# Six of seven key groups of the later pairs staged split and turned by VectorE

## What is computed

```python
qp = jnp.einsum('bsd,de->bse', q, Wq) + bq        # q = layernorm(x), (8, 64, 512)
kp = jnp.einsum('bsd,de->bse', k, Wk) + bk        # k = v = ctx_1024, (8, 1601, 512)
vp = jnp.einsum('bsd,de->bse', v, Wv) + bv
logits = jnp.einsum('bqe,bke->bqk', qp, kp) * scale
attn = jax.nn.softmax(logits, axis=-1)
return jnp.einsum('bqk,bke->bqe', attn, vp)
```

## Time and profile before

| | |
|---|---|
| median of three runs | 350.5 us |
| profiled execution | 349.09 us, span 347.4 us, mean granted clock 0.986 |
| TensorE matmul busy | 315.8 us (91%), 1940 instructions |
| VectorE busy | 161.4 us (46%), 349 instructions |
| ScalarE busy | 89.1 us (26%) |
| GpSimd busy | 77.6 us (22%) |
| moved by DMA | 74.29 MB in 61221 packets, 214 GB/s over the span |
| packets under 2 KB | 40070 |

### The profile page before, as it was taken

How to read it: one execution, slowest core, us unless ns; L and a number is a source line. 1 busy time by engine, 2 the same in 40 slices (tenths; PEclk the granted TensorE clock), 3 DMA queues, 4 the chain that set the end, 5 groups by cost and what they waited for, 6 DMA issues and landing times. The chain is left out here.

```text
span 347.4 us, 5470 instructions
## 1 busy us (share of the span) xinstructions
PE 315.8 (91%) x1940; PEld 174.8 (50%) x1940; DVE 161.4 (46%) x349; ACT 89.1 (26%) x207; POOL 77.6 (22%) x84
## 2 busy tenths in 40 slices
PE   0997988999999899999899999999999998789992
PEld 0786654743545544454554454543475577433330
DVE  3205149505463857183767437442362647034331
ACT  1233210145113463221335321152312501011010
POOL 4000012660015200221500201321325210601212
PEclk9999998899999999999999999999999999999998
DMA  7999999999999897999796999680696053730110
GB/s 252 387 351 176 184 372 359 190 190 364 298 197 300 166 158 255 298 196 354 109 169 106 352 245 234 231 358 0 235 422 252 0 184 123 222 141 31 44 41 9
DMA packets 61221, 74.29 MB, mean 214 GB/s; under 512 B 3174, under 2 KB 40070, under 8 KB 60176
## 3 DMA queue, kind: packets, MB, share of 16 engines
q1 hardware_dynamic: 59648, 69.23, 75.8%
q0 software_dynamic: 1552, 4.78, 3.9%
HBM read 70.85 MB, written 3.67 MB: 215 GB/s over the span
## 5 line engine op out<-in xcount | busy, mean ns | idle before, releaser
L1182 PE MATMUL ST<-CTX_sb,PR_sb 128*64 128x512 f32 (+1 forms) x208 | 47.7, 599 | 1.1 <-ACT PR_sb L338 1.1
L784 DVE STREAM_TRANSPOSE CT_sb<-FF_sb 128x1024 f32<-128x1024 f32 x36 | 42.4, 1220 | 11.6 <-DMA FF_sb<-ctx 10.0
L1157 PE MATMUL SC<-CT_sb,qcurP_sb 128*64 128x256 f32 x288 | 38.6, 398 | 3.3 <-DVE CT_sb L784 3.3
L1157 PEld LDWEIGHTS SC<-CT_sb,qcurP_sb 128*64 128x64 f32 x288 | 19.2, 140 | 17.9 <-issue 7.3
L1182 PEld LDWEIGHTS ST<-CTX_sb,PR_sb 128*64 128x64 f32 (+1 forms) x208 | 14.1, 136 | 24.3 <-issue 23.5
L1082 PE MATMUL A<-AW_sb,normT_sb 128*128 128x512 f32 x48 | 22.0, 600 | 0.0
L511 POOL TENSOR_TENSOR rn_sb<-ss_sb,nhalf_sb 128x16 f32<-128x16 f32 x4 | 11.6, 2905 | 35.9 <-DVE ss_sb L863 35.9
L1075 PE MATMUL TR<-ident_sb,CTX_sb 128*128 128x128 f32 (+1 forms) x128 | 15.9, 266 | 1.3 <-DVE CT_sb L331 1.1
L1125 PE MATMUL A<-AO_sb,WQK_sb 128*128 128x128 f32 (+1 forms) x64 | 16.2, 413 | 0.7 <-ACT AO_sb L611 0.7
L1075 PEld LDWEIGHTS TR<-ident_sb,CTX_sb 128*128 128x128 f32 (+1 forms) x128 | 12.9, 141 | 7.5 <-issue 5.6
L1326 PE MATMUL SC<-ident_sb 128*128 128x128 f32 x130 | 16.4, 278 | 0.0
(11 more groups left out here) (242 smaller groups left out, 489.9 us busy)
## 6 DMA issues: line engine op xcount, KB each, us to landing
CTX_sb<-ctx SPq DMA_DIRECT2D x24, 1024.0 KB, 10.4
FF_sb<-ctx SPq DMA_DIRECT2D x80, 128.0 KB, 6.9
FF_sb<-ctx SPq DMA_DIRECT2D x32, 256.0 KB, 8.0
CTX_sb<-wgu SPq DMA_DIRECT2D x4, 1024.0 KB, 9.6
CTX_sb<-wdn SPq DMA_DIRECT2D x5, 512.0 KB, 12.6
FF_sb<-wgu SPq DMA_DIRECT2D x2, 1024.0 KB, 6.2
rows<-XR_sb SPq DMA_DIRECT2D x3, 512.0 KB, 10.3
CTX_sb<-ctx SPq DMA_DIRECT2D x8, 130.0 KB
```

The source lines that it names most:

```text
L784: v.transpose(ctxT[:, pos % 2, k, :, :].rearrange("p c (b r) -> p b c r", r=Q), split[:, k, at:at + BLOCKS, :].rearrange("p b (c r) -> p b ...
L1157: last = t_.matmul(out[q, :], (qcurP if split_group else qcur)[:, c, q], ctxT[:, pos % 2, k, c, 0:n], start=(c == 0), stop=(c == DC - 1))
L1182: last = t_.matmul(ST[q, :], probs[0:w, t, q], ctxb[0:w, k, t, :], start=(t == 0), stop=(t == KT - 1))
```

## The change

The later pairs take the groups in the order 0 to 6, and group 0 is split too: only the tail is turned by TensorE. The slot of a group is its number modulo three. The first pair keeps three split and four unsplit groups, renumbered: 3, 4, 5, 6 unsplit, then 0, 1, 2 split, and its chunks 0 and 1 swap their places in the loads. Before a pair, groups 0 and 1 are loaded when all but the last split group of the pair before are turned, group 2 when that one is turned too; in `load_pair`, groups 3 and 4 are issued where 4 and 5 were, then chunk 3, then, once group 2 is turned, group 5 in a part of its own, and chunk 2 last.

```diff
-SLOT_OF = {1: 0, 2: 1, 3: 2, 4: 0, 5: 1}
-SPLIT_PARTS = ((1, 2), (3,), (4,), (5,))
+SLOT_OF = {0: 0, 1: 1, 2: 2, 3: 0, 4: 1, 5: 2}
+SPLIT_PARTS = ((0, 1), (2,), (3,), (4,), (5,))
...
-FIRST = Order((0, 4, 5, 6, 1, 2, 3), (1, 2, 3))
-NEXT = Order((1, 2, 0, 3, 4, 5, 6), (1, 2, 3, 4, 5))
+FIRST = Order((3, 4, 5, 6, 0, 1, 2), (0, 1, 2))
+NEXT = Order((0, 1, 2, 3, 4, 5, 6), (0, 1, 2, 3, 4, 5))
...
             def next_split(p):
 
-                sp.wait_ge(s["keysT_made"], split_turned(p, order_of(p).split.index(3) + 1))
+                done = len(order_of(p).split)
+                sp.wait_ge(s["keysT_made"], split_turned(p, done - 1))
+                settle(sp)
+                load_split(p + 1, 0)
+                sp.wait_ge(s["keysT_made"], split_turned(p, done))
                 settle(sp)
                 load_split(p + 1, 1)
-                sp.wait_ge(s["keysT_made"], split_turned(p, len(order_of(p).split)))
-                settle(sp)
-                load_split(p + 1, 0)
...
                 load_split(p, 2)
                 load_split(p, 3)
                 load_chunk(p, 3)
+                sp.wait_ge(s["keysT_made"], split_turned(p, 3))
+                settle(sp)
+                load_split(p, 4)
                 load_chunk(p, 2)
...
-            for c in (0, 2, 3):
+            for c in (1, 2, 3):
                 load_chunk(0, c)
...
-            load_chunk(0, 1)
+            load_chunk(0, 0)
```

## The result

The changed kernel took 357.4 us (median of 4 runs, 354.1 to 359.8) against 350.1 us for the kernel before on the same chip: ratio 1.015, 95% interval 1.009 to 1.021. The medians and ranges of this document are of all runs, while a ratio is of the runs within 1.5% of the fastest of their kernel, here without the one of 359.8 us. The changed kernel is slower; whether by as much as 2% is open. A second measurement of the same kernel gave 358.5 us and 1.020 (1.015 to 1.026). The profiled execution took 357.34 us, its span is 355.6 us, 8.2 more than before.

A forecast was written before the change was run, and what follows sets the result against it. TensorE was taken as the bound from 60 to 235 us. Terms 3.3 + 1.2 + 0.6 + 0.8 + 1.5 = +7.4 on the profiled 349.1 gave 356.5; with 1.4 for the median 357.9, forecast 358, range 352.5 to 363.

The forecast's parts named there:

- the three transfer terms: Later pairs' loads: group 3 late +1.2, gates and what follows +0.6, group 5 late +0.8 us.
- Removed transposes: TensorE, tiles 0 and 1 of three pairs: 16 transposes a pair fewer, 2.0 us a pair, 6.0 us in all.
- The chain y, turn, statistics, a2: VectorE's group 2 turn between x1 and statistics delays a2: +1.1 us a pair, +3.3 over three pairs.
- Late group 3: First later pair: VectorE waits 3.6 us for group 3, normT follows, TensorE waits for q: +1.2 us.
- the gates behind it: First later pair: group 4's turn delays q's squares, k norm and gates, then group 5 and resonance steps: about +0.6 us.
- TensorE is through the v projection at 102.1: First later pair: step by which TensorE, done with v at 102.1, waits for q until 103.3: +1.2 us.
- Late group 5: Group 5's own part behind the tail chunk lands about 224 us in the third pair, TensorE waits: +0.8 us.
- The clock, one fall: New TensorE waits, 3.2 us idle in 4.2 a pair, bring one half-clock fall: +1.5 us (none to 4.5).
- The edits costed at nothing: First pair's renumbering, chunk 2 issued some 7 us later, earlier load of next pair's first two groups: no cost.
- B: Rival: only the chain costs, transfers land early enough and the clock holds: 353.8 us, chance 0.17.
- C: Rival: clock falls in every pair, or group 3 is late in later pairs too: 361 us, chance 0.18.
- D: Rival: a2 chain has room, removed transposes count in full; a2 must be 2 us plus turn old: 344.5, chance 0.10.

The follow-up runs named there:

- experiment 8: Experiment 6's kernel with SyncE issuing chunk 2 only behind the next pair's groups 0 and 1: 347.91 us, ratio 0.989 to the kernel before.
- experiment 10: Changed kernel with only the load order new (parts ahead of chunks 0 and 1, chunk 2 behind the next pair's groups): 355.16 us, ratio 1.013.
- Experiment 2: Kernel before plus four stream transposes of 128x512 into dead buffers on VectorE, behind y in the later pairs: 357.53 us, ratio 1.018.
- experiment 1: Changed kernel with VectorE turning the group at position 2 ahead of y: 355.57 us, ratio 1.014 to the kernel before.
- experiment 3: Changed kernel without group 5's loads and the waits for them (its scores are wrong): 355.05 us, ratio 1.013 to the kernel before.
- experiment 5: Changed kernel with 4 and 6 filler matmuls in TensorE's two waits: 359.12 us, ratio 1.021; changed kernel again beside it: 358.54 us, 1.020.
- experiment 6: Experiment 1's kernel with the parts of groups 3, 4, 5 and the tail issued ahead of chunks 0 and 1: 350.41 us, ratio 0.998.
- experiment 4: Changed kernel with 10 and 14 filler matmuls of 128x128 in TensorE's two waits of each later pair: 361.70 us, ratio 1.031.
- experiment 9: Experiment 8's kernel with TensorE scoring the second half of group 2 ahead of the transpose of a2: 348.87 us, ratio 0.989.

## Why the prediction was right

Forecast 358, measured 357.4; the profiled sum was +7.4, measured +8.2. The total is nearer than its terms, and that is partly luck: the chain came out as forecast, the three transfer terms (2.6 us) cost TensorE nothing in the profiled execution, and the clock cost 4.2 us there instead of 1.5.

- **Removed transposes, 6.0 us.** Right: 48 fewer, 42 stream transposes. Experiments 8 and 10 show what they are worth once the chain is out of the way and the loads are in time.
- **The chain y, turn, statistics, a2: +3.3.** Right in mechanism and size. Forecast: waits of 1.35 and 1.85 us, a2 on TensorE 5.8 us after x1, +1.1 a pair. Measured: 1.19, 1.65 (once 1.72), 5.8 us (97.48 against 91.72), +1.04 to +1.11. Experiment 2 puts about the same work there without the change and loses 1.9 a pair; experiment 1 moves it away and turns +1.04 into −1.1 up to a2; experiments 3 and 10 keep it with less or earlier traffic, and it stays.
- **Late group 3 and the gates behind it, +1.2 and +0.6.** In the profiled execution VectorE's wait was there (2.83 us instead of 3.6, and 2.00 more for group 4), but its effect on TensorE was not: the step that failed is "TensorE is through the v projection at 102.1". At half clock it was through at 105.5. In the filled kernel's execution of experiment 5, which began early and held the clock, both waits appeared (1.01 and 1.14 us), in experiment 1 too (0.72 and 1.03 us), and in the second profile of the changed kernel, which began late, neither. So the terms belong to some executions and not to all.
- **Late group 5, +0.8.** Not in the first profile (0.56 us of waiting, 0.63 before), where SyncE issued the part in 5.08 us and I had taken 7.3: I priced its issues by half of a stretch of sixteen that stood behind two whole chunks. It was there in the second profile (1.51 us), where SyncE took 6.23 us, and at its worst in experiment 1 (2.54 us).
- **The clock, one fall, +1.5.** Mis-sized: two falls, 2.8 and 1.4 us, in the first profile; none in the pairs in the second and in experiment 3; one of 2.8 in experiment 10. The Trainium skill, TensorE: Matmul & The Clock Gate, What's actually happening, has idleness as the trigger. The traces agree that falls follow the waits; nothing in them says why the same two waits (1.19 and 1.65 us) brought one in 3 of the 12 pairs of these four profiles and not in the others. The row that the forecast took its one fall from was no surer: the same wait of 2.08 us in the first pair brought a fall in the kernel before and none in the changed one, as TensorE's timelines show, before and after. Why stays open.

```profile
53.22 2.40 PE L1157 MATMUL SC<-CT_sb,qcurP_sb 128*64 128x256 f32 x16 [2.08 <-DVE CT_sb L784]
```

```profile
53.88 1.95 PE L1161 MATMUL SC<-CT_sb,qcurP_sb 128*64 128x256 f32 x16 [2.08 <-DVE CT_sb L788]
```

- **The edits costed at nothing.** The first pair's renumbering and chunk 2's later issue left no wait in the profiles of the changed kernel; the 0.6 us ahead of the first start are within what that start varies by, so whether the renumbering has a part in them is not shown.
- **Rivals.** B (only the chain, 353.8) describes the pairs of experiment 3, whose median is 3.7 us above its kernel before, and of experiment 10 but for the clock. C (the clock in every pair) happened in no profiled execution. D (faster) fell at the point named for it: a2 was not 2 us old. Yet its amount was partly to be had, once the turn was moved and the loads put in another order: the removed work was real, and the place of what replaced it ate it.

In the median, the loss is 5 to 7 us (by the ratio 1.015 and by the medians); 3.1 of it are the chain; the other 2 to 4 are what is left, and by the profiles they are clock falls and late transfers. How these two divide could not be settled, since the slow clock hides the late transfer: TensorE at half clock came to q only when normT was there.

## What to carry to other kernels

When work is moved from the bound engine to one with time to spare, look not at its busy share but at the instruction behind which it will stand and at the chain that it delays; 2.36 us in the one place between x1 and the statistics cost more than the 2.0 us of TensorE that it saved, in each of three pairs. If the order is at fault, move the new work ahead of the wait it stands behind. Then look again at the load queue: here each repair (experiments 1, 6, 8) uncovered the next late transfer, and the gain came only with both, the turn moved and the loads issued in the order of need.

## What the runs showed of the hardware

- A 128x128 float32 matmul used as filling is recorded as two and took 0.24 us back to back (ten of them, 20 records, from 93.49 us to the next start at 95.92, experiment 4).
- Eight DMAs of one split group took SyncE 4.0 to 6.9 us to issue where they stood behind the tail chunk (changed kernel, both profiles, and experiment 1). Sixteen took 13.1 to 16.8 us where whole chunks had been issued just before, and 7.72 us in the first later pair of experiment 10, where none had. These are SyncE's issues in the changed kernel and in experiment 10. An issue time measured behind a full queue is not the price of the issue.

```profile
83.85 16.29 SPq L359 DMA_DIRECT2D FF_sb<-ctx  x16
```

```profile
83.32 7.72 SPq L359 DMA_DIRECT2D FF_sb<-ctx  x16
```

- Alike kernels began the later pairs at 84.7 to 85.4 us or at 87.3 to 87.7. The late ones had the half clock at another place of the first pair: in the second profile of the changed kernel a step of 3.73 us (L1305) took 5.04. The 23 runs of the kernel before beside experiments 8 to 10 lie in two bunches about as far apart, 349.2 to 350.1 us and 351.0 to 352.5. With falls and late transfers on top, the runs of the changed kernel spread over 5.7 us (354.1 to 359.8), those of the kernel before over 3.5 (349.1 to 352.7). A single profile attributes such differences to places that the next profile does not show.
